# A batch-major sequence buffer between the token mixing and the bidirectional LSTM

## The reference

```python
# token mixing, per batch
q, k, v = x @ Wq + bq, x @ Wk + bk, x @ Wv + bv
y = ((d_gamma * (q @ k.T)) @ v) @ Wo + bo
h = where(y >= 0, y, prelu_a * y)
# LSTM autoencoder on layernorm(h), hidden size 128
h_fwd = lstm(x @ Wf + bf, Uf)                # last state only
h_bwd = lstm(x @ Wb + bb, Ub, reverse=True)  # last state only
dec   = lstm(concat(h_fwd, h_bwd) @ Wd + bd, Ud, return_sequences=True)
h = h + dec @ Wo + bo
# top-2-of-8 experts (gelu, 64 -> 128 -> 64) on layernorm(h)
h = h + experts(layernorm(h))
```

## Time and profile before

| | us |
|---|---|
| median of 3 runs | 4182.74 (4173.4 to 4185.41) |
| the profiled execution's own time | 4172.61 |
| its span | 4170.8 |
| setup and first preparation | 0 to about 43 |
| token mixing | to about 494 |
| encoder | 494 to about 2300 |
| decoder and experts | to the end |

### The profile page before, as it was taken

One profiled execution on the slowest core, in us unless ns is written; L12 is line 12 of the kernel. 1 busy time (PEld: TensorE's weight loads), 2 busy tenths in 40 slices (PEclk: granted clock), 3 DMA queues, 4 the chain that ended last, 5 costly groups with the idle time before them and its releaser, 6 DMA issues. The chain is left out here.

```text
span 4170.8 us, 170266 instructions
## 1 busy us (share of the span) xinstructions
PE 3797.3 (91%) x65013; PEld 2633.8 (63%) x65029; DVE 3214.5 (77%) x23274; ACT 1880.3 (45%) x9834; POOL 84.6 (2%) x131
## 2 busy tenths in 40 slices
PE   6888799999999999999999788888888888888888
PEld 3232377777777777777777555555555565555554
DVE  5777699999999999999999666666666666666665
ACT  3333455555555555555555333433334433334433
POOL 7100000000000000000000000000000000000000
PEclk8888899999999999999999899999999999999999
DMA  3000000000000000000000000000000000000000
GB/s 85 16 21 21 9 3 4 4 4 3 4 4 4 4 4 4 4 4 4 4 4 4 5 7 6 7 6 7 7 6 7 6 7 7 7 6 7 6 7 7
DMA packets 49627, 34.66 MB, mean 8 GB/s; under 512 B 37661, under 2 KB 46877, under 8 KB 48806
## 3 DMA queue, kind: packets, MB, share of 16 engines
q1 hardware_dynamic: 48806, 23.77, 2.2%
HBM read 15.37 MB, written 8.39 MB: 6 GB/s over the span
## 5 line engine op out<-in xcount | busy, mean ns | idle before, releaser
L728 PE MATMUL bank<-xs,ident 128*128 128x128 f16 x18680 | 1817.3, 219 | 0.0
L728 PEld LDWEIGHTS bank<-xs,ident 128*128 128x128 f16 x18680 | 1132.5, 97 | 62.8 <-issue 40.5
L737 PEld LDWEIGHTS bank<-enc_hi,u_lo 128*128 128x128 f16 x8192 | 339.1, 96 | 367.3 <-DVE enc_hi L784 367.2
L737 PE MATMUL bank<-enc_hi,u_lo 128*128 128x16 f16 x8192 | 528.5, 173 | 27.8 <-DVE enc_hi L784 4.5
L749 ACT ACTIVATE ifg_cell_dec<-bank 128x48 f32<-128x48 f32 x1024 | 216.2, 211 | 712.7 <-PE bank L741 712.7
L763 DVE SCALAR_TENSOR_TENSOR terms_dec<-ifg_cell_dec 128x32 f32<-128x32 f32 x1024 | 197.3, 193 | 434.6 <-ACT ifg_cell_dec L749 422.9
L737 PEld LDWEIGHTS bank<-ring_hi,u_lo 128*128 128x128 f16 x4096 | 174.4, 97 | 540.4 <-DVE ring_hi L784 533.1
L741 PE MATMUL bank<-enc_lo,u_hi 128*128 128x16 f16 x8192 | 504.6, 170 | 1.4
L737 PE MATMUL bank<-enc_hi,u_hi 128*128 128x16 f16 x8192 | 500.2, 169 | 0.0
L737 PE MATMUL bank<-ring_hi,u_lo 128*128 128x16 f16 x4096 | 264.4, 173 | 222.9 <-DVE ring_hi L784 212.0
L756 ACT ACTIVATE tanh_cell_fwd<-twice_cell_fwd 128x16 f32<-128x16 f32 x1024 | 221.4, 216 | 414.4 <-DVE twice_cell_fwd L769 414.4
(11 more groups left out here) (269 smaller groups left out, 8067.3 us busy)
## 6 DMA issues: line engine op xcount, KB each, us to landing
g_rows<-tok_d_gamma_batched_dram SPq DMA_DIRECT2D x8, 512.0 KB, 7.6
x_rows<-in_x_dram SPq DMA_DIRECT2D x16, 256.0 KB, 3.1
kept_h<-tok_ln_h SPq DMA_DIRECT2D x32, 128.0 KB, 2.1
res<-kept_h SPq DMA_DIRECT2D x32, 128.0 KB
out_dram<-sums SPq DMA_DIRECT2D x32, 128.0 KB
raw_wd<-in_L_attn_Wd_dram SPq DMA_DIRECT2D x2, 256.0 KB
raw_experts<-in_L_ffn_W_dram SPq DMA_DIRECT2D x2, 256.0 KB
raw_u<-in_L_attn_Uf_dram SPq DMA_DIRECT2D x1, 256.0 KB
```

The costliest lines, as they stand in the source:

```text
L728: nc.tensor.matmul(spare, m.ident16[:], m.xs[:, COLS:COLS + P], start=False, stop=True, skip_group_check=True)
L737: nc.tensor.matmul(z[k], w[:, g, :], h_hi, start=False, stop=False, skip_group_check=True)
```

## The change

`xs` becomes `[P, B, T]`: batch outermost, the 1024 steps of a batch next to each other, no padding. ACT's copy of a batch writes 1024 neighbouring f16. A fill's moving operand is 8 steps of 16 batches; the batches are 2 KB apart in the buffer, and as the batch is the inner index of the result, each of its 128 columns lies 2 KB from the one before it (or back to the first batch). `pe_idle` reads 128 neighbouring columns as before, at another place. The two memsets of the padding are gone.

```diff
-        m.xs = sb("xs", [P, T * B + 2 * COLS], F16)
+        m.xs = sb("xs", [P, B, T], F16)
...
-                nc.gpsimd.memset(m.xs[:, 0:COLS], 0.0)
-                nc.gpsimd.memset(m.xs[:, COLS + T * B:], 0.0)
...
-                        S.copy(m.xs[:, COLS:COLS + T * B].rearrange("p (t b) -> p t b", b=B)[:, :, b],
-                               m.bank[7][:].bitcast(F16)).then_inc(s_nk, 1)
+                        S.copy(m.xs[:, b, :], m.bank[7][:].bitcast(F16)).then_inc(s_nk, 1)
...
-        nc.tensor.matmul(spare, m.ident16[:], m.xs[:, COLS:COLS + P], start=False, stop=True, skip_group_check=True)
+        nc.tensor.matmul(spare, m.ident16[:], m.xs[:, 0, 0:P], start=False, stop=True, skip_group_check=True)
...
-                    first = COLS + STEPS * B * (CHUNKS - 1 - q if d else q)
-
-                    nc.tensor.matmul(z, m.w_hi[d][:, g, :], m.xs[:, bass.ds(first, STEPS * B)],
+                    first = STEPS * (CHUNKS - 1 - q if d else q)
+                    x = m.xs[:, :, first:first + STEPS].rearrange("p b t -> p t b")
+
+                    nc.tensor.matmul(z, m.w_hi[d][:, g, :], x,
                                      start=(k in (0, 3)), stop=False, skip_group_check=True)
-                    nc.tensor.matmul(z, m.w_lo[d][:, g, :], m.xs[:, bass.ds(first, STEPS * B)],
+                    nc.tensor.matmul(z, m.w_lo[d][:, g, :], x,
                                      start=False, stop=False, skip_group_check=True)
```

## The result

| | us |
|---|---|
| before, median of 4 runs | 4183.44 (4173.4 to 4185.41) |
| after, median of 4 runs | 4252.61 (4247.89 to 4256.56) |
| ratio | 1.0167, 95% interval 1.0152 to 1.0183 |
| profiled execution after: own time, span | 4251.58, 4249.8 |

The forecast was 4112, so the time went the other way. The prediction's first rival (the fills come out from under their cover) had said so, at 4265 for four times the column time; 4252.61 was measured.

The account below looks back on a forecast made before the run. ACT's copy stalls DVE and PE in mixing; an ACT and DVE ring paces the encoder. 4172.6 - 49 - 12.6 - 5.2 + 1.8 = 4107.6 us, 4117.7 on the median, middle 4112; range 4092 to 4270.

Parts of the forecast that it names:

- first rival: Encoder half steps with a fill: stepped reads outlast PE's waiting, costing 1016 x (2D - 0.18) us; 4265 or about 4750; chance 0.27.
- cover: Encoder: the 180 to 190 ns PE waits per half step, hiding added PE work up to D = 90 ns.
- The fills: Encoder: two of each fill's three matmuls read columns 2 KB apart; 110 ns more per half step, hidden, so 0.
- D: Added time of one fill matmul with a stepped operand: bounded by 0 and 435 ns, taken as 55 ns.
- The copy and its stall: Mixing: ACT's copy into xs falls from 4.495 to 1.012 us, ending DVE's 3.52 us wait; 14 x 3.5 = 49 us gained.
- The clock: Mixing, behind PE's pause: full clock kept, L485 at 1.08 instead of 1.97 us; 14 x 0.9 = 12.6 us, bounds 0 and 22.
- The bare first fills: Eight fills ahead of the encoder's first step, with no wait to hide them: 16 x 0.11 = 1.8 us lost.
- The memsets: Two memsets of 0.30 us each at 4 us, long before mixing: removing them counts 0.
- low clock stays: Mixing: the pause goes but PE still drops to 1.2 GHz, so 12.6 us is missing; about 4125 us; chance 0.08.
- the likeliest case: Whole kernel: the forecast itself, 4112 us with its own range 4092 to 4125; chance 0.56.

## Why the prediction was wrong

**The step that failed** is one term of *The fills*: "I take that it doubles: D = 55 ns". It measured 0.16 us. The sum had 110 ns under a cover of 180 ns and so counted nothing; it was 325 ns, some 141 ns of it past the cover in each of 1016 half steps, and the encoder became 141 us longer. The first rival said this, with its place, its formula and, for D = 165, its price of 152 us; 141 to 143 were measured. So the mechanism stood in the text and the choice between the ends was wrong. It had no row of a stepped read behind it, only the remark that PE's own row was nearer in kind than ACT's write, and that is no evidence on steps. The chance of 0.27 was too low for a term of unknown size whose break-even lay at 2.2 times the plain price of an element added (122 ns on 55).

**A new line at each column.** One read per 16 bytes cost 160 to 175 ns more for 128 columns, two still cost 55, four cost nothing. So the warning that the prediction took from the Trainium skill (Advanced Engine Details and Errata, "SBUF Cachelines") was right in that a different line at each access costs, but at least two hits on a line, which it asks for, are not enough here. Two remarks beside it were wrong. The columns are not each on a line of its own: eight lie on one, but never two in a row are read from it. And the trace's write, which the prediction took as agreeing, doesn't follow the rule: two f16 on a line cost 1028 ns as runs of two and 2447 ns as steps of 8 bytes.

**The cover** of 0.18 us was right: 0.182 and 0.184 us by two experiments, and its end at 2D = 180 ns agrees with 160 to 165 ns in all being free.

**The copy and its stall**: 1.007 us instead of the 1.012 forecast, DVE's wait gone. **The clock** behind it came back, and its term was too small: a batch takes 22.35 us (from copy to copy, 121.44 to 367.28 us for eleven of them), before it was 27.3 (257.74 to 285.04). Of these 4.9 us 3.5 are the stall, so by subtraction 1.4 are the clock's, nearer the upper bound of 1.6 than the 0.9 taken. Against that nearly nothing was gained up to the second copy (it starts at 121.44, before at 121.76). The whole was 70.5 us, forecast 66.8.

That the clock would stay was luck in part. The reason given was that pauses of 0.4 to 0.9 us occur in every slot at a clock of 1.00, with 280 to 286 as the proof. But PE is busy for 6.00 of the 6.00 us there, and between 265 and 286 PE has no such pause in the trace. What shows it are the changed kernel's own pauses: 0.48 and 1.19 us in a batch, at a clock of 1.00 from 144 to 389 us. (The clock of 1.00 "in the stall" is that of a window ending 1 us before the stall does; from 262 to 264, at the end of the stall before it, the mean is 0.84.)

**The bare first fills**, 1.8 us, cost 1.6: from the first of them to the first matmul with the state it is 4.15 us, before it was 2.51. **The memsets and the rival "low clock stays"**: nothing seen of either.

**Two sums** are off, and neither bears on the outcome: with ACT's price the rival comes to 4112 + 701 = 4813 and not to 4750, and the lower end of the likeliest case, by what it names, is 4107.6 - 9.4 = 4098 and not 4092.

## What to carry to other kernels

When a layout moves a step from a write to a read, count the f16 that share 16 bytes and are accessed in a row, on each side: here four were free for a matmul's operand (three were not tried) and two neighbours for ACT's write, and a blocked layout (here pairs of steps inside the batch) can give both their due. Where the price of an access is in no row, measure it before choosing between bounds; here one kernel with a stepped fill would have turned the forecast round. And before a layout is changed to shorten an instruction, see whether it only stands in the wrong place of its engine's order: moving the copy by one slot gave 44 of the 71 us.

## What was not expected of the hardware

A stepped operand costs time, and hardly more of it at the low clock. In the first fills of the encoder the granted clock is 0.50 in both kernels. A plain fill takes 0.32 us there instead of 0.165. A stepped fill takes 0.52 us (4.15 us for eight) instead of 0.49, and the starts in these rows are 0.20 and 0.21 us apart, as at the full clock:

```profile
423.65 0.38 PE L824 MATMUL bank<-xs,w_hi 128*128 128x128 f16 x1 [1.36 <-PEq L428]
...
423.85 0.40 PE L826 MATMUL bank<-xs,w_lo 128*128 128x128 f16 x1
...
424.06 0.28 PE L828 MATMUL bank<-ones,bias 128*128 128x128 bf16 x1
```

```profile
423.60:427.00 3.40, 3.35 (x20) 2.27 (x21) 0.58 (x10) 1.59 (x3) 0.00 (x0) 0.50 0.02 5
```

That is 0.205/128 = 1.6 ns for each column that is read from another 16 bytes than the one before it, at either clock (up to 0.23/128 = 1.8 ns in the fills that follow at the low one). A result stepped by 192 bytes in PSUM costs about 50 ns per 128 columns, and a write of 128x1024 f16 by ACT in pairs 64 bytes apart costs 1.03 us, where single ones 32 bytes apart cost 4.5 us.
